# Expert loop of a routed mixture of experts: one turned tile per block, other distances between the steps of a block

## The reference

```python
x = x + 0.5 * ffn(layernorm(x))
x = x + attn(layernorm(x))
x = x + 0.5 * ffn(layernorm(x))

def ffn(xf):                                  # 32 experts, six chosen for each token
    scores = sigmoid(xf @ gate_weight.T)
    combine = weights of the 6 chosen experts, 0 elsewhere
    for e in range(32):
        g, u = xf @ gu[e][:128].T, xf @ gu[e][128:].T
        routed += combine[:, e] * (silu(g) * u @ dn[e].T)
    return routed + shared expert of width 256
```

## Time and profile before

| | us |
|---|---|
| median of 3 runs (1592.07 to 1594.62) | 1593.38 |
| the profiled execution's own time | 1589.19 |
| its span, from the first to the last instruction | 1587.4 |
| first expert loop, first row transposes to last down product | 276.9 to 645.0 |
| second expert loop, the same | 1104.1 to 1473.1 |

### The profile page before, as it was taken

The page is one execution under the profiler, slowest core; times in us unless marked ns, Lnnn a source line. Parts: engine busy times, 40 slices in busy tenths (PEclk is TensorE's granted clock), DMA queues, the critical chain, the costliest instruction groups (busy, mean ns, idle before and its releaser), DMA issues.

```text
span 1587.4 us, 50394 instructions
## 1 busy us (share of the span) xinstructions
PE 1371.1 (86%) x9950; PEld 1152.5 (73%) x9951; DVE 1071.4 (67%) x5500; ACT 659.6 (42%) x2374; POOL 901.8 (57%) x955
## 2 busy tenths in 40 slices
PE   6867761999999999699799999962999999999895
PEld 5756651888888888565477777742888888888884
DVE  5676563677777777367368788873777777777576
ACT  3333320555555555100277677630555555555110
POOL 3777776466656666200007677775566666656686
PEclk9777775999999999899799899965999999999998
DMA  9953333555555554476003333343555555554799
GB/s 310 401 220 129 129 129 122 165 182 172 175 175 180 178 173 149 146 265 228 1 16 126 125 140 129 130 145 125 167 179 177 177 174 176 169 177 136 237 303 307
DMA packets 156140, 275.45 MB, mean 174 GB/s; under 512 B 29094, under 2 KB 108475, under 8 KB 156096
## 3 DMA queue, kind: packets, MB, share of 16 engines
q1 hardware_dynamic: 112000, 157.39, 32.0%
q0 software_dynamic: 39936, 113.33, 19.4%
q10 hardware_dynamic: 4160, 4.19, 0.8%
HBM read 147.90 MB, written 135.27 MB: 178 GB/s over the span
## 4 chain that ended last, share of the span: by engine, by line
PE 41%; POOL 24%; issue 18%; DVE 6%; DMA 5%; ACT 3%; POOLq 1%; DVEq 0%; SPq 0%; ACTq 0%
PE ps L640 34%; POOL dispatch_rows L566 11%; POOL answers L608 10%; DMA ans<-answers 4%; PE ps L741 4%; PE ps L770 2%; POOL dispatch_rows L592 1%; ACT ans L1219 1%; POOL xres L622 1%; DVE smax L1718 1%; DVE yb L1646 1%; DVE stats L1296 1%; ACT xnt L1084 0%; DMA answers<-yb,didx 0%; ACT ans L1178 0%
## 5 line engine op out<-in xcount | busy, mean ns | idle before, releaser
L608 POOL DMA_INDIRECT answers<-yb,didx x448 | 440.5, 983 | 316.5 <-issue 197.3
L640 PE MATMUL ps<-wgu,xbt 128*128 x1792 | 463.9, 382 | 0.0
L592 POOL DMA_INDIRECT dispatch_rows<-blk,idx x192 | 190.4, 992 | 259.0 <-issue 240.2
L640 PEld LDWEIGHTS ps<-wgu,xbt 128*128 128x128 f32 x1792 | 307.6, 192 | 23.8
L1519 DVE SCALAR_TENSOR_TENSOR hb<-ps,wcol,sg 128x128 f32<-128x128 f32 x448 | 157.1, 351 | 167.1 <-ACT sg L1131 111.1
L640 PE MATMUL ps<-wdn,hbt 128*128 x896 | 267.0, 380 | 1.8 <-ACT hbt L1135 1.8
L1507 DVE SCALAR_TENSOR_TENSOR picked<-iota_e,etab,blk 128x32 f32<-128x32 f32 x896 | 190.4, 250 | 67.7 <-DMA blk<-dispatch_rows 32.1
L566 POOL DMA_INDIRECT dispatch_rows<-blk,idx x192 | 187.1, 975 | 80.7 <-issue 57.9
L1131 ACT ACTIVATE sg<-ps 128x128 f32<-128x128 f32 x448 | 124.2, 277 | 234.8 <-PE ps L640 234.7
L741 PE MATMUL ps<-ident,blk 128*128 128x128 f32 x896 | 173.0, 275 | 34.5 <-DMA blk<-dispatch_rows 34.5
L1125 ACT COPY xbt<-ps 128x256 f32<-128x256 f32 x448 | 168.2, 376 | 70.3 <-PE ps L741 70.0
(11 more groups left out here) (193 smaller groups left out, 2052.8 us busy)
## 6 DMA issues: line engine op xcount, KB each, us to landing
blk<-dispatch_rows SPq DMA_DIRECT2D x448, 160.0 KB
ans<-answers SPq DMA_DIRECT2D x64, 512.0 KB, 3.8
ans<-answers SPq DMA_DIRECT2D x64, 256.0 KB, 3.8
wgu<-in_gate_up SPq DMA_DIRECT2D x32, 256.0 KB
answers<-yb,didx POOLq DMA_INDIRECT x448
dispatch_rows<-blk,idx POOLq DMA_INDIRECT x384
dispatch_rows<-padt SPq DMA_DIRECT2D x32, 160.0 KB
wdn<-in_down SPq DMA_DIRECT2D x16, 256.0 KB
```

Of the source, the lines that this page charges most:

```text
L592: pool.indirect_dma_start(out=rows_dram, out_offset=bass.IndirectOffsetOnAxis(ap=idx[:, q, k:k + 1], axis=0), in_=rows[:, q, :], in_offset ...
L608: pool.indirect_dma_start(out=answers_dram, out_offset=bass.IndirectOffsetOnAxis(ap=didx[:, q:q + 1], axis=0), in_=yb[:, q, :], in_offset= ...
L640: return nc.tensor.matmul(out_, lhs, rhs, start=start, stop=stop)
```

## The change

It alters the turn of a block in five ways.

- The transposes of the rows of n+2 and of `hb` n-3 now form one group, `turn(n + 2)`, at the head of turn n. They write one bank (TH, two of them in turn): 256 columns for the rows and 128 for `hb`. ScalarE copies all 384 columns at once to `turned`, which lies in the upper half of `ans` and has four slots; silu follows that copy.
- The down product of turn n is that of block n-5 (before, n-2); its left operand comes out of `turned`.
- GU has four banks in place of two; `sg` and `hb` have four slots. `xbt` and `hbt` go. TensorE keeps the expert numbers in four registers, with one load a turn as before.
- Every block has its own column of `wcol` and `dcol`, so `pick` no longer waits for `h`; the columns are addressed by a register.
- Eight turns are peeled at the start and the last go on to NB + 5.

```diff
@@ -192,14 +192,12 @@
         rows = blk
-        xbt = sb("xbt", [P, 2, D])
-        sg = sb("sg", [P, 2, I])
-        hb = sb("hb", [P, 2, I])
-        hbt = sb("hbt", [P, 2, I])
+        sg = sb("sg", [P, 4, I])
+        hb = sb("hb", [P, 4, I])
         yb = sb("yb", [P, 4, D])
         picked = sb("picked", [P, 2, E])
-        wcol = sb("wcol", [P, 4])
-        dcol = sb("dcol", [P, 4])
+        wcol = sb("wcol", [P, NB])
+        dcol = sb("dcol", [P, NB])
         didx = sb("didx", [P, 4], I32)
@@ -209,7 +207,7 @@
         red = sb("red", [P, D])
         two_sums = [yb[:, 2 * j:2 * j + 2, :] for j in range(2)]
-        third_sum = [red[:], sg[:].rearrange("p j i -> p (j i)")]
+        third_sum = [red[:], sg[:, 0:2, :].rearrange("p j i -> p (j i)")]
         xn = yb
@@ -248,6 +246,9 @@
         means = flat[:, TOPK * D * 2 - 2 * 4 * D:]
         vv = sb("vv", [P, 2, D])
+        turned = ans[:, 1, :].rearrange("p (q n) -> p q n", q=4)
         smax = sb("smax", [P, HL])
         nmax = sb("nmax", [P, HL])
         psum_ = sb("psum_", [P, HL])
@@ -307,14 +308,12 @@
                 self.bc = s("tb_bc")
                 self.tab = s("tb_tab")
                 self.ld = [s(f"ex_ld{q}") for q in range(4)]
-                self.tx = s("ex_tx")
-                self.xt = s("ex_xt")
+                self.th = s("ex_turned")
+                self.cp = s("ex_copied")
                 self.pick = s("ex_pick")
                 self.gu = s("ex_gu")
                 self.sg = s("ex_sg")
                 self.h = s("ex_h")
-                self.ht = s("ex_ht")
-                self.hts = s("ex_hts")
                 self.d = s("ex_d")
                 self.y = s("ex_y")
                 self.take = s("ex_take")
@@ -454,7 +453,7 @@
                     first = sp.value_load(itab[0:1, bass.ds(n + 2 * P, 1)], min_val=0, max_val=E * CAP - P)
                     if not peeled:
-                        sp.wait_ge(s.tx, n - 3)
+                        sp.wait_ge(s.th, n - 3)
                         sp.wait_ge(s.pick, n * 2 - 6)
                     sp.dma_start(blk[:, q, :], rows_dram[bass.ds(first, P), :]).then_inc(s.ld[q], 16)
             body(0, True)
@@ -501,7 +500,7 @@
                                  ).then_inc(s.ans[k][j], 16)
-            sp.wait_ge(x.tx, NB)
+            sp.wait_ge(x.th, NB)
             sp.wait_ge(x.pick, 2 * NB)
             for q in range(4):
                 load_tokens(q, q)
@@ -721,69 +720,68 @@
                 m = mm(ps[:, 1, h * P:(h + 1) * P], ones[:], diag_twice[:, h, :])
             m.then_inc(s.bc, 1)
-        TX, GU, HT, DN = 0, 2, 4, 6
+        GU, TH, DN = 0, 4, 6
+        AHEAD = 2
+        BEHIND = 5
         def pe_experts(pe, s):
-            now = [pe.alloc_register(f"expert_now{j}_{s.n}") for j in range(2)]
-            old = [pe.alloc_register(f"expert_old{j}_{s.n}") for j in range(2)]
+            now = [pe.alloc_register(f"expert_now{q}_{s.n}") for q in range(4)]
+            old = [pe.alloc_register(f"expert_old{q}_{s.n}") for q in range(4)]
             pe.wait_ge(s.tab, 1)
             pe.wait_ge(ld_exp, 16 * 3 * (NT // 2))
             pe.reg_load(now[0], itab[0:1, 0:1])
-            pe.reg_mov(now[1], 0)
-            pe.reg_mov(old[0], 0)
-            pe.reg_mov(old[1], 0)
-            def tx(n, q):
-                pe.wait_ge(s.ld[q], 16 * (n // 4 + 1) if isinstance(n, int) else n * 4 + (16 - 4 * q))
-                for c in range(KC):
-                    m = pe.transpose(ps[:, TX + q % 2, c * P:(c + 1) * P], blk[:, q, c * P:(c + 1) * P], ident[:])
-                m.then_inc(s.tx, 1)
+            for q in range(1, 4):
+                pe.reg_mov(now[q], 0)
+            for q in range(4):
+                pe.reg_mov(old[q], 0)
+            def turn(t, q, m=None):
+                if m is None or BEHIND <= t:
+                    pe.wait_ge(s.h, t - BEHIND + 1)
+                    o = pe.transpose(ps[:, TH + q % 2, D:D + P], hb[:, (q - BEHIND) % 4, :], ident[:])
+                if m is None or t < NB:
+                    pe.wait_ge(s.ld[q], 16 * (t // 4 + 1) if isinstance(t, int) else t * 4 + (16 - 4 * q))
+                    for c in range(KC):
+                        o = pe.transpose(ps[:, TH + q % 2, c * P:(c + 1) * P], blk[:, q, c * P:(c + 1) * P], ident[:])
+                o.then_inc(s.th, 1)
             def step(n, q, m=None):
-                j = q % 2
+                pe.wait_ge(s.cp, n + 1)
+                if m is None or n + AHEAD < NB + BEHIND:
+                    turn(n + AHEAD, (q + AHEAD) % 4, m)
                 if m is None or n < NB:
-                    e = pe.snap(now[j], min_val=0, max_val=E - 1)
-                    pe.wait_ge(s.xt, n + 1)
+                    e = pe.snap(now[q], min_val=0, max_val=E - 1)
                     for c in range(KC):
-                        g = mm(ps[:, GU + j, 0:2 * I], xbt[:, j, c * P:(c + 1) * P],
+                        g = mm(ps[:, GU + q, 0:2 * I], turned[:, q, c * P:(c + 1) * P],
                                wgu[:, c, bass.ds(e * (2 * I), 2 * I)], start=(c == 0), stop=(c == KC - 1))
                     g.then_inc(s.gu, 1)
+                pe.reg_mov(old[q], now[(q + 1) % 4])
                 if m is None or n + 1 < NB:
-                    pe.reg_mov(old[1 - j], now[1 - j])
-                    pe.reg_load(now[1 - j], itab[0:1, bass.ds(n + 1, 1)])
-                elif n + 1 == NB:
-                    pe.reg_mov(old[1 - j], now[1 - j])
-                if m is None or n >= 2:
-                    e2 = pe.snap(old[j], min_val=0, max_val=E - 1)
-                    pe.wait_ge(s.hts, n - 1)
-                    positive(pe, s.y, n - 3)
-                    mm(ps[:, DN + j, 0:D], hbt[:, j, :], wdn[:, bass.ds(e2 * D, D)]).then_inc(s.d, 1)
-                if m is None or 1 <= n < NB + 1:
-                    pe.wait_ge(s.h, n)
-                    pe.transpose(ps[:, HT + 1 - j, 0:P], hb[:, 1 - j, :], ident[:]).then_inc(s.ht, 1)
-                if m is None or n + 2 < NB:
-                    tx(n + 2, (q + 2) % 4)
-            tx(0, 0)
-            tx(1, 1)
+                    pe.reg_load(now[(q + 1) % 4], itab[0:1, bass.ds(n + 1, 1)])
+                if m is None or n >= BEHIND:
+                    e2 = pe.snap(old[(q + 2) % 4], min_val=0, max_val=E - 1)
+                    positive(pe, s.y, n - BEHIND - 1)
+                    mm(ps[:, DN + 1 - q % 2, 0:D], turned[:, q, D:D + P],
+                       wdn[:, bass.ds(e2 * D, D)]).then_inc(s.d, 1)
+            for t in range(AHEAD):
+                turn(t, t, m=0)
             return step
         def pe_experts_run(pe, s):
             step = pe_experts(pe, s)
-            for n in range(4):
+            for n in range(8):
                 step(n, n % 4, m=0)
-            with pe.Fori(1, NB // 4 - 1) as g:
+            with pe.Fori(2, NB // 4 - 1) as g:
                 for q in range(4):
                     step(g * 4 + q, q)
-            for n in range(NB - 4, NB + 2):
+            for n in range(NB - 4, NB + BEHIND):
                 step(n, n % 4, m=0)
         def pe_combine(pe, s):
@@ -1119,34 +1117,29 @@
             pairs_by_two(act, body, NT // 2)
         def act_experts(act, s):
-            def xt_copy(n, j):
-                act.wait_ge(s.tx, n + 1)
-                positive(act, s.gu, n - 1)
-                act.copy(xbt[:, j, :], ps[:, TX + j, 0:D]).then_inc(s.xt, 1)
-            def step(n, j, m=None):
+            def copied(t, q, m=None):
+                act.wait_ge(s.th, t + 1)
+                a = D if m is not None and t >= NB else 0
+                b = D if m is not None and t < BEHIND else D + P
+                act.copy(turned[:, q, a:b], ps[:, TH + q % 2, a:b]).then_inc(s.cp, 1)
+            def step(n, q, m=None):
+                copied(n + AHEAD, (q + AHEAD) % 4, m)
                 if m is None or n < NB:
                     act.wait_ge(s.gu, n + 1)
-                    positive(act, s.h, n - 1)
-                    act.activation(sg[:, j, :], ps[:, GU + j, 0:I], ACT.Silu).then_inc(s.sg, 1)
-                if m is None or n >= 1:
-                    act.wait_ge(s.ht, n)
-                    positive(act, s.d, n - 2)
-                    act.copy(hbt[:, 1 - j, :], ps[:, HT + 1 - j, 0:P]).then_inc(s.hts, 1)
-                if m is None or n + 2 < NB:
-                    xt_copy(n + 2, j)
-            xt_copy(0, 0)
-            xt_copy(1, 1)
-            step(0, 0, m=0)
-            step(1, 1, m=0)
-            step(2, 0, m=0)
-            step(3, 1, m=0)
-            with act.Fori(2, NB // 2 - 1) as pair:
-                step(pair * 2, 0)
-                step(pair * 2 + 1, 1)
-            for n in range(NB - 2, NB + 1):
-                step(n, n % 2, m=0)
+                    positive(act, s.h, n - 3)
+                    act.activation(sg[:, q, :], ps[:, GU + q, 0:I], ACT.Silu).then_inc(s.sg, 1)
+            for t in range(AHEAD):
+                copied(t, t, 0)
+            for n in range(8):
```

(47 more changed lines are left out.)

## The result

| | median us | runs |
|---|---|---|
| kernel before | 1588.34 | 18 (1585.96 to 1594.62) |
| changed kernel | 1595.62 | 18 (1594.0 to 1601.8) |

The ratio is 1.0048, 95% interval 1.0038 to 1.0058: 7.6 us slower, 6.0 to 9.2. The profiled execution of the changed kernel took 1596.1 us, its span is 1594.3, against 1589.19 and 1587.4.

A forecast was written before the change was run, and what follows sets the result against it. TensorE's streamed columns bound the loops. Start and end terms, 2 x (0.9 + 1.4) = +4.6 us, took the profiled 1589.2 to 1593.8; on the 1593.4 median that put the forecast at 1598.0, range 1592.5 to 1604.

The forecast's parts named there:

- Steady state: Body of both expert loops: TensorE's order of kinds is unchanged and it stays fully busy, so 0 us.
- Rows' cover: Row loads inside the loops: slack before the rows are turned falls from 2.57 to 0.83 us, nothing charged.
- Rival C: Inside the loops: rows come late in every turn, each 0.1 us costing 45 us, 1640 and up; 7% chance.
- Start: Start of each loop: rows wanted ahead of gate/up 0 and short first turns leave TensorE waiting, +0.9 us (0.3 to 2.0).
- End: End of each loop: six down products, queued scatters and waits for `yb` slots delay the last scatter, +1.4 us (0.3 to 3.0).
- No change: Loop ends: the last scatter's stall is swallowed by the queue ahead of it, +1.2 us in all, 1594.6; 27% chance.
- Signs: In the trace: gate/up 223 ends near 641.4, last scatter near 651.2, sum stage and second loop shifted 2.3 us each.
- three signs of being wrong: In the trace: TensorE idle for `blk` inside a loop; last scatter at or before 649; clock below full after 283.

The follow-up runs named there:

- idle matmuls: Unneeded TensorE matmuls ahead of both loops; 16 and 15: kernel before 0.9988, changed kernel 1.0048; 13 and 10: 0.9992 and 1.0033.
- four-back run: Changed kernel with the down product four blocks back in place of five: 1593.75 us against 1590.44 for the kernel before, ratio 1.0026.
- run with own slots: Changed kernel with the last four blocks copied to separate slots, their scatters behind GpSimd's loop: 1595.9 us against 1589.22 for the kernel before, ratio 1.0041.

## Why the prediction was right

The direction and the range were right: slower, 1595.62 inside 1592.5 to 1604. But 1598.0 was the sum of 1593.38 and 4.6, and both were off in opposite ways. More runs put the kernel before at 1588.34, and the change costs 7.6 (6.0 to 9.2). That 1598.0 came within 2.4 us is in part luck: from 1588.34 the same sum would have said 1592.9.

- **Steady state, 0.** The beat and the full clock held, 40.00 of 40 in the same window. Over the first loop it was not quite zero: TensorE misses 0.26 us between 476 and 516, and 0.25 between 296 and 306.
- **Rows' cover, 2.57 to 0.83 us, no charge.** From the trace, landing to first use is 2.7 us at the median before and 0.86 and 0.95 after, with 0.04 as its least. The size was right. The step "it stays positive, so I charge nothing" is not quite true: a median that thin lets single loads through (0.25 us twice in the first loop), and they cost tenths of a microsecond. The run with rows one ahead and the down product three back has the same thin cover and 0.2 us more idle time in both loops together. Rival C, late in every turn, did not come.
- **Start, +0.9 (0.3 to 2.0).** Gate/up 0 came 1.06 us later behind the first transpose. Two more transposes at half clock are 0.43 of it, and 0.6 is idle, as worked out. All in all idle and half clock cost 1.65 us per loop (3.1 and 0.2 in the two loops), the two row waits above among them. This is the term that was mis-sized; the mean is inside its range, the first loop outside. Its spread is the clock's, which rose 7.76 and 5.53 us into the loops, where it had been 4.16 and 6.43. Over all runs without idle matmuls it rose after 4.2 to 6.8 us in the old order and after 4.6 to 7.8 in changed ones, so how much of it is the change and how much chance was not separated. Shown is the late first gate/up: forced into the kernel before, it made the loops 1.65 and 0.16 us longer.
- **End, +1.4 (0.3 to 3.0).** Measured +1.24: the last scatter at 9.73 behind the last gate/up, where 9.9 was worked out. The four-back run (8.44) and the run with own slots (8.64) change it by the amounts of the queue and of the slots. The slots came free 2.2 us after their scatters' starts, and the last scatter of the first loop landed in 2.12 again, as in the earlier trace rows. By the fit of the Trainium skill ("DMA: Bandwidth & Descriptors", Anatomy of one DMA — SWDGE (gpsimd) path) it is 2.3, an estimate; the measurement decides, and 2.12 stands for these. But the sum took one landing for all, and single ones take longer: 3.32 for the last scatter of the second loop, which adds 1.2 us to the 2.5 of both ends, and 3.69 for a slot where the idle matmuls ran, which by itself makes the tail 10.6.
- **"No change", 27%.** Its mechanism, a stall swallowed by the queue, exists: it is what the run with own slots shows, with a tail of 8.64. In the change itself the waits for slots of `yb` kept it from happening.
- **Signs.** The last gate/up ended at 644.53 and not near 641.4, the last scatter started at 654.26 and not 651.2. Of these 3 us, 1.0 is an earlier stage, and the rest the start term of the first loop, 3.1 in place of 0.9. The second loop began 5.5 us later and not 2.3. And two of the three signs of being wrong came: TensorE idle for `blk` inside a loop (298.74), and a clock below full after 283 (0.50 until past 285). They point at the start term and the cover, which are off in size by 2.2 us and by tenths, and not at the end term, which is right by its parts.

The loops give 5.8 us, and the medians 7.6 with 6.0 as the low end. The late landing behind the second loop makes it 7.0, inside the interval of the medians. That this is the difference is not tested; it rests on single traces: kernels with nearly the same loops measured 1.0033 to 1.0048, and other stages vary from run to run too.

## What to carry to other kernels

A deeper software pipeline on an engine that is already busy at every moment has nothing to win in the body of the loop and pays at its ends: each block that the last step falls further back adds one block's work behind the last product, and an input that is wanted before the first product instead of behind it makes the first product wait. Count the loop's two ends before its body: how many results will stand in line behind the last one, what the slowest of the serial steps does with that line, and how many slots hold them. Where those slots are all in use, a single transfer that lands late is on the path. And where a move cuts the cover of a load to a fraction of a microsecond, charge something for it, since single loads use it up long before the median does.
